# Differential attention, the first of two layers: three of eight query tiles transposed by VectorE instead of two, and the softmax ratio moved from VectorE to ScalarE

## The chip, the cores and the metric

The kernel runs on one core of one Trainium2 chip. The metric is device time in microseconds of one execution. A core has five engines that run their own instruction streams and wait for each other through semaphores: TensorE (PE in the profile; PEld is its loading of weights), VectorE (DVE), ScalarE (ACT), GpSimd (POOL) and SyncE (SP), which here only issues DMAs.

## The reference

Two transformer layers over X of shape (2, 1024, 128). The change touches only the attention of the first layer, a differential attention with 16 heads of width 64:

```
Q1, Q2 = halves of X Wq + bq      K1, K2 = halves of X Wk + bk      V = X Wv + bv
P  = softmax(Q1 K1' / 8) - lam * softmax(Q2 K2' / 8)
O  = P V ;  Y = concat_heads(O) Wo + bo ;  layer norm, times 0.2, and so on
```

After it come a mixture-of-experts feed-forward part, a second attention (16 heads of width 8) and a gated feed-forward part. They are the same in both kernels.

## The kernel before

**Tiling.** The first layer is a loop over `n` from 0 to 31: `n = 2 * head + batch`. Each n has 8 steps `s`, one for each tile of 128 queries. In a step, TensorE computes two fills of scores (`scores(n, s, p)`, p = 0 for Q1K1, p = 1 for Q2K2), each 128 queries x 1024 keys in two PSUM banks. A fill is numbered v = 2s + p within n. Three pairs of banks serve as a ring (`ring(v)`), and a fill waits until the exponential that read its pair two or three fills ago is done. Once per n the ring skips a place so that the pair 0 takes the projection of Q for the next n (`project_q`), and the pair 2 the output product. Q and K are split in a high and a low float16 part (`high_q`, `high_k` on ScalarE write the high part from PSUM, `low_q`, `low_k` on VectorE the rest), and a fill is three products of them.

**The way of a tile.** VectorE takes the negative maximum of a fill over the keys (`maximum`, line 1152). ScalarE takes the exponential with that as bias and leaves the row's sum (`exponent`, line 847). When both exponentials of a tile are there, VectorE takes the reciprocals of the two sums (`weigh`, line 1159) and the ratio rho = lam * sum1 / sum2 (line 1161). GpSimd scales the second exponential by rho and subtracts it from the first (`subtract`, lines 655 and 656). The result, still to be divided by sum1, is transposed so that it can be multiplied by V:
- six of the eight tiles (`BY_PE`) by TensorE, in two runs of four 128x128 transposes into one PSUM bank (`turn(n, s, i)`, line 1585), each run evacuated by ScalarE (`keep_t`, line 858). Tile s is turned in step s + 3.
- two tiles, 0 and 2 (`BY_DVE`), by VectorE in 32x32 blocks (`turn_blocks`, line 1204), in steps 3 and 5; SyncE stores the blocks to DRAM and loads them back in their places (`store_blocks`, `load_turned`).

**The values.** The product with V of n - 1 (`values`, line 1599) runs as 8 pieces in steps 3 to 6 of n: `PIECES` gives pieces 0, 1, 2 to step 3, piece 3 to step 4, pieces 4, 5, 6 to step 5 and piece 7 to step 6. In step 3 they stand between the fills v6 and v7. VectorE divides by the first sum, spread over partitions by DMA (`normalise`, step 7).

**Order.** Every engine's order is written out by hand in loops over n and s; there is no planner. In a step, VectorE's order before the change is: maximum of the first fill, `weigh` of the tile before, maximum of the second fill, then what else the step has: in step 2 `low_q(n + 1)` behind the second maximum, in steps 3 and 5 `turn_blocks`. Ahead of the first maximum stand `normalise` in step 7 and `keep_v` in step 0. `low_k` stands in steps 1 and 2 between the maxima. The fill v7 waits for `low_q(n + 1)`, as it uses the pair that held Q's projection. ScalarE's order in a step is: `keep_t` of one half, first exponential, `keep_t` of the other half, second exponential, with `high_k` in steps 1 and 2 and `high_q` (line 871) in step 2. GpSimd's order is the eight `subtract`, and behind tile 4 of every even n `part_w`, the five small operations that prepare the next head's weights; in the first four n it has further preparation (`prepare`). An exponential of tile s + 4 writes into the buffer of tile s, so it waits until that tile is turned.

Of the kernel before, what the change touches and what calls it, by code (L numbers as in the profile page):

```python
# [28 lines left out]
def two_layers(nc, a, out):  # L29
    ctx = ExitStack()  # L30
    with ctx:
# [308 lines left out]
        BY_DVE = (0, 2)  # L340
# [42 lines left out]
        def _(sp):  # L383
# [81 lines left out]
            def store_blocks(n, i):  # L465

                sp.wait_ge(s_bt_ok, 2 * n + i + 1)
                if n >= 1:
                    sp.wait_ge(s_ptr_dma[(n - 1) % 2], 64 * ((n - 1) // 2 + 1))
                for j in range(4):  # L470
                    sp.dma_start(ptd[i].rearrange("(m p) (b c) -> p m b c", m=4, b=4)[:, :, j, :],
                                 stage[i][32 * j:32 * j + 32, :].rearrange("p (m c) -> p m c", m=4)).then_inc(s_ptw_dma, 16)

            def load_turned(n, i):

                sp.wait_ge(s_ptw_dma, 64 * (2 * n + i + 1))
                if n >= 2:
                    sp.wait_ge(s_pv_mm, n - 1)
                elif n == 1:
                    sp.wait_ge(s_wprep_ev, 6)  # L480
                at = 4 * BY_DVE[i]
                for k in range(2):
                    sp.dma_start(PT[2 * n % 3][k][:, at:at + 4, :, :], ptd[i].rearrange(
                        "p (b k c q) -> p b k c q", b=4, k=2, c=4)[:, :, k, :, :]).then_inc(s_ptr_dma[n % 2], 16)
# [8 lines left out]
            for n in range(-1, last0 + 1):  # L493
# [28 lines left out]
                if own:  # L522
                    store_blocks(n, 0)
                    spread_r(n, 0)
                    load_turned(n, 0)
                    store_blocks(n, 1)
                    load_turned(n, 1)
# [89 lines left out]
        def _(pool):  # L617
# [32 lines left out]
            def subtract(n, s):  # L650

                q = 8 * n + s
                e1, e2 = E1[s % 4], E2[s % 4]
                pool.wait_ge(s_rho_ok, q + 1)
                link(P.tensor_scalar(e2, e2, rho[:, s:s + 1], 1.0, ALU.mult, ALU.mult))  # L655
                P.tensor_tensor(e1, e1, e2, ALU.subtract).then_inc(s_sub_ok, 1)  # L656
# [62 lines left out]
            scale_q(0)  # L719
            for n in range(last0):  # L720
# [82 lines left out]
        def _(act):  # L803
# [33 lines left out]
            def exponent(n, s, p):  # L837
# [3 lines left out]
                if p == 0:  # L841
                    prev, tile = (n, s - 4) if s >= 4 else (n - 1, s + 4)
                    if tile in BY_DVE:
                        act.wait_ge(s_bt_ok, 2 * prev + BY_DVE.index(tile) + 1)
# [5 lines left out]

            def keep_t(n, s, i):
# [3 lines left out]
                if s in (1, 4) and i == 0:  # L855
                    at_least(act, s_pv_mm, n - 1 + half)
# [17 lines left out]
            for n in range(-1, last0 + 1):  # L874
                prv, own, nxt = n >= 1, 0 <= n < last0, n + 1 < last0
                for s in range(8):
# [19 lines left out]
                    if own:  # L896
                        exponent(n, s, 0)
                    if 3 <= s < 6 and n == 0:
# [178 lines left out]
        def _(dve):  # L1077
# [77 lines left out]
            def weigh(n, b, s):  # L1155
# [41 lines left out]
            def turn_blocks(n, i):  # L1197

                dve.wait_ge(s_sub_ok, 8 * n + BY_DVE[i] + 1)
# [19 lines left out]
            for n in range(-1, last0):  # L1219
                prv, own, nxt = n >= 1, 0 <= n < last0, n + 1 < last0  # L1220
                for s in range(8):
# [8 lines left out]
                    if n == 0 and s == 1:  # L1230
                        dve.wait_ge(s_ld_l0, 48)
# [280 lines left out]
        def _(pe):  # L1512
# [75 lines left out]
            def values(n, j):  # L1588
# [4 lines left out]
                if j == 0:  # L1593
                    pe.wait_ge(s_ptr_dma[n % 2], 64 * (n // 2 + 1))
# [97 lines left out]
            PIECES = {3: (0, 1, 2), 4: (3,), 5: (4, 5, 6), 6: (7,)}  # L1692
# [429 lines left out]
```

## Time and profile before

Three runs took 1572.45, 1575.74 and 1575.19 us: the median is 1575.19. The profiled execution took 1573.77 us; its trace has a span of 1572.0 us from the first to the last instruction.

| | busy us | share of the span |
|---|---|---|
| TensorE (matmul) | 1439.6 | 92% |
| VectorE | 1376.4 | 88% |
| ScalarE | 1198.3 | 76% |
| GpSimd | 1003.8 | 64% |

The mean granted clock of TensorE is 0.967 of full speed. The chain of work that ended last lies for 53% on TensorE, 14% on ScalarE, 13% on VectorE and 7% on GpSimd; 11% of it is issue. The first layer's attention takes about the first 1060 us of the span, and GpSimd's work lies almost all in it. In timelines, the first number is the start in us from the span's start, the second the busy time; a pair in square brackets is the idle time of that engine before it and what released it. Successive operations on an engine overlap a little, so what an operation costs is better read from one start to the next.

### The profile page before, as it was taken

The page shows a single profiled execution, that of the slowest core. Times are in us where ns is not written, and L with a number is a line of the kernel's source. Part 1 is how long each engine was busy: PE and PEld are TensorE (multiplying, and loading weights), DVE is VectorE, ACT ScalarE, POOL GpSimd, SP SyncE. Part 2 cuts the span into 40 slices and gives each one's busy share as a digit, 9 for nine tenths or more (in the row PEclk, how much of TensorE's full clock was granted, in tenths as well). Part 3 has the DMA queues.
Part 4 walks back from the last instruction along what each step waited for, and adds up shares of the span by engine and source line. Part 5 has one row for each costly group of instructions (what it writes and reads, how often), then busy time and mean ns, then how long its engine had stood idle before and what let it go on. Part 6 is the DMA issues. An engine that isn't in the chain of part 4 may idle for free.

```text
span 1572.0 us, 28031 instructions
## 1 busy us (share of the span) xinstructions
PE 1439.6 (92%) x10243; PEld 588.5 (37%) x10243; DVE 1376.4 (88%) x2107; ACT 1198.3 (76%) x1911; POOL 1003.8 (64%) x727
## 2 busy tenths in 40 slices
PE   5899999999999999999999999986685999999985
PEld 1434443344434443344334433434541222222223
DVE  6798998999899989999999989988687999999947
ACT  4787888888888888888888888874342888888882
POOL 2999998898898988989889889880032011111112
PEclk9999999999999999999999999997696999999997
DMA  4243433343244323433343333420000110000001
GB/s 126 76 105 92 106 86 82 102 112 90 78 103 110 96 77 104 109 92 85 91 107 105 83 91 93 114 68 1 1 22 21 31 35 15 16 16 16 16 16 34
DMA packets 154641, 110.80 MB, mean 70 GB/s; under 512 B 31381, under 2 KB 142906, under 8 KB 154506
## 3 DMA queue, kind: packets, MB, share of 16 engines
q1 hardware_dynamic: 154378, 108.99, 26.5%
q8 instruction: 82, 1.34, 0.4%
q14 instruction: 53, 0.43, 0.1%
q0 software_dynamic: 128, 0.03, 0.0%
HBM read 53.82 MB, written 34.87 MB: 56 GB/s over the span
## 4 chain that ended last, share of the span: by engine, by line
PE 53%; ACT 14%; DVE 13%; issue 11%; POOL 7%; DMA 1%; SPq 0%; POOLq 0%; ACTq 0%; DVEq 0%
PE PS L1573 14%; PE PS L1585 10%; PE PS L1599 9%; ACT ering L847 7%; PE PS L1980 4%; POOL ering L656 3%; DVE nmx L1152 2%; PE PS L1942 2%; DVE region L1172 2%; PE PS L1632 2%; PE PS L1964 2%; ACT region L871 2%; DVE mxp L1479 2%; ACT ering L1059 2%; POOL ering L655 2%
## 5 line engine op out<-in xcount | busy, mean ns | idle before, releaser
L1152 DVE TENSOR_REDUCE nmx<-PS 128x1 f32<-128x1024 f32 x512 | 620.1, 1216 | 54.4 <-PE PS L1574 53.5
L847 ACT ACTIVATE ering<-PS,nmx 128x1024 f32<-128x1024 f32 x512 | 570.6, 1116 | 109.6 <-DVE nmx L1152 109.5
L656 POOL TENSOR_TENSOR ering<-ering 128x1024 f32<-128x1024 f32 x256 | 604.2, 2360 | 21.4
L1573 PE MATMUL PS<-region 64*128 64x512 f16 x1536 | 405.1, 381 | 20.4 <-ACT ering L847 14.5
L1574 PE MATMUL PS<-region 64*128 64x512 f16 x1536 | 405.2, 381 | 0.0
L655 POOL TENSOR_SCALAR ering<-ering,rho 128x1024 f32<-128x1024 f32 x256 | 287.3, 1122 | 95.2 <-DVE rho L1161 94.5
L1479 DVE TENSOR_REDUCE mxp<-PS 128x2 f32<-128x1024 f32 x256 | 304.2, 1222 | 34.3 <-PE PS L1964 29.9
L1059 ACT ACTIVATE ering<-PS 128x1024 f32<-128x1024 f32 x256 | 259.6, 1024 | 70.0 <-PE PS L1942 64.1
L1585 PE MATMUL PS<-ident,ering 128*128 128x128 f32 x1536 | 251.5, 286 | 15.6 <-ACT t L858 8.1
L1585 PEld LDWEIGHTS PS<-ident,ering 128*128 128x128 f32 x1536 | 161.6, 141 | 201.7 <-issue 73.8
L1573 PEld LDWEIGHTS PS<-region 64*128 64x128 f16 x1536 | 112.6, 94 | 261.3 <-ACT ering L847 110.2
L1980 PE MATMUL PS<-ering,acc 128*32 128x256 f32 x2048 | 160.5, 391 | 5.0 <-ACT ering L1059 1.5
L761 POOL TENSOR_TENSOR on<-osb,rcp 128x512 f32<-128x512 f32 x16 | 20.4, 1276 | 155.3 <-DMA rcp<-scr 155.3
L1574 PEld LDWEIGHTS PS<-region 64*128 64x128 f16 x1536 | 112.5, 94 | 0.0
L1599 PE MATMUL PS<-t,region 128*64 128x512 f32 x224 | 108.3, 608 | 0.0
L1599 PE MATMUL PS<-region 128*64 128x512 f32 x216 | 104.5, 609 | 0.0
L847 ACT ACTIVATION_READ_ACCUMULATOR ering<-PS,nmx 128x1 f32 x512 | 104.1, 203 | 0.0
L858 ACT ACTIVATE t<-PS 128x512 f32<-128x512 f32 x132 | 78.9, 598 | 28.0 <-PE PS L1585 27.2
L858 ACT ACTIVATE region<-PS 128x512 f32<-128x512 f32 x124 | 74.1, 598 | 20.5 <-PE PS L1585 19.7
L1204 DVE STREAM_TRANSPOSE t<-ering 128x1024 f32<-128x1024 f32 x64 | 79.0, 1234 | 0.0
L1161 DVE TENSOR_SCALAR rho<-sums,rr,cols 128x1 f32<-128x1 f32 x256 | 69.9, 273 | 9.3
L779 POOL TENSOR_TENSOR yT<-yT,yc 128x512 f32<-128x512 f32 x12 | 15.2, 1270 | 88.5 <-ACT yc L1040 88.5
(301 smaller groups left out, 1876.2 us busy)
## 6 DMA issues: line engine op xcount, KB each, us to landing
ptd<-t SPq DMA_DIRECT2D x256, 128.0 KB, 2.4
region<-region SPq DMA_DIRECT2D x64, 256.0 KB, 3.5
t<-ptd SPq DMA_DIRECT2D x44, 256.0 KB, 3.5
region<-ptd SPq DMA_DIRECT2D x44, 256.0 KB, 3.5
va<-ptd SPq DMA_DIRECT2D x20, 256.0 KB, 3.4
acc<-ptd SPq DMA_DIRECT2D x20, 256.0 KB, 3.5
osb<-scr SPq DMA_DIRECT2D x32, 128.0 KB, 3.3
rcp<-scr SPq DMA_DIRECT2D x32, 128.0 KB, 3.3
```

The source lines that it names most:

```text
L655: link(P.tensor_scalar(e2, e2, rho[:, s:s + 1], 1.0, ALU.mult, ALU.mult))
L656: P.tensor_tensor(e1, e1, e2, ALU.subtract).then_inc(s_sub_ok, 1)
L847: A.activation((E1, E2)[p][s % 4], PS[:, bank:bank + 2, :].rearrange("p a b -> p (a b)"), ACT.Exp, bias=nmx[:, 2 * s + p:2 * s + p + 1], s ...
L858: A.activation(PT[(2 * n + half) % 3][i][:, at:at + 4, :, :].rearrange("p b k q -> p k b q"), TRB.rearrange("p (k b q) -> p k b q", k=4, b ...
L1059: A.activation(ering[:, c % 8, :, :], PS[:, at:at + 2, :], ACT.Exp, scale=SCALE1).then_inc(s_exps1, 1)
L1152: V.tensor_reduce(nmx[:, 2 * s + p:2 * s + p + 1], PS[:, bank:bank + 2, :].rearrange("p a b -> p (a b)"), AX.X, ALU.max, negate=True).then ...
L1479: V.reduce_max(part[:, 2 * hp:2 * hp + 2, qt, kh:kh + 1], PS[:, at:at + 2, :], AX.X).then_inc(s_maxed1, 1)
L1573: MM(PS[:, bank, :], top[0:64, ql, q], KT[b][0:64, p, kl, :], start=(j == 0), stop=(j == 2))
L1574: mm = MM(PS[:, bank + 1, :], bottom[64:128, ql, q], KT[b][64:128, p, kl, :], start=(j == 0), stop=(j == 2))
L1585: mm = TR(TRB[:, j * 128:j * 128 + 128], E1[s % 4][:, k * 128:k * 128 + 128], ident[:, :])
L1599: mm = MM(MISC[64 * half:64 * half + 64, :], vt, PT[(2 * n + half) % 3][j // 4][:, :, j % 4, :], start=(j == 0), stop=(j == 7))
L1980: mm = MM(OT[32 * i:32 * i + 32, at], vst[:, n % 2, k, i, :], ering[:, c % 8, i // 2, at], start=(k == 0 and half == 0), stop=(k == 7 and ...
```

## The change

- `BY_DVE` becomes (0, 1, 2): tile 1 too is transposed by VectorE, in step 4, and no longer by TensorE and ScalarE. The two staging buffers and DRAM buffers are used in turn by the three tiles, with the waits that this takes.
- The ratio leaves VectorE's `weigh`. ScalarE makes sum1 / sum2 (`ratio`), behind the first exponential of the next step. Lambda is applied by GpSimd, as second factor of its scaling, where there was 1.0.
- `low_q(n + 1)` moves from the end of step 2 to step 3, behind the first maximum and ahead of `weigh`.
- `PIECES` moves piece 4 of the values from step 5 to step 4.
- The wait for the constants (`s_ld_l0`) moves from VectorE's first steps to GpSimd, ahead of its loop.

```diff
-        BY_DVE = (0, 2)
+        BY_DVE = (0, 1, 2)
...
             def store_blocks(n, i):
-                sp.wait_ge(s_bt_ok, 2 * n + i + 1)
-                if n >= 1:
-                    sp.wait_ge(s_ptr_dma[(n - 1) % 2], 64 * ((n - 1) // 2 + 1))
+                c = len(BY_DVE) * n + i
+                sp.wait_ge(s_bt_ok, c + 1)
+                if c >= 2:
+                    sp.wait_ge(s_ptr_dma[c % 2], 32 * (c // 2))
...
                     store_blocks(n, 0)
                     spread_r(n, 0)
                     load_turned(n, 0)
-                    store_blocks(n, 1)
-                    load_turned(n, 1)
+                    for i in range(1, len(BY_DVE)):
+                        store_blocks(n, i)
+                        load_turned(n, i)
...
-                link(P.tensor_scalar(e2, e2, rho[:, s:s + 1], 1.0, ALU.mult, ALU.mult))
+                link(P.tensor_scalar(e2, e2, rho[:, s:s + 1], cols[:, LAM:LAM + 1], ALU.mult, ALU.mult))
...
+            pool.wait_ge(s_ld_l0, 48)
             for n in range(last0):
...
+            def ratio(n, s):
+                act.wait_ge(s_rr_ok, 8 * n + s + 1)
+                A.activation(rho[:, s:s + 1], sums[:, s, 0:1], ACT.Identity, scale=rr[:, n % 2, 1, s:s + 1],
+                             bias=0.0).then_inc(s_rho_ok, 1)
...
                     if own:
                         exponent(n, s, 0)
+                    if own if s else prv:
+                        ratio(n if s else n - 1, (s + 7) % 8)
...
                 V.reciprocal(rr[:, b, :, s], sums[:, s, :]).then_inc(s_rr_ok, 1)
-                dve.wait_ge(s_rr_ok, q + 1)
-                V.tensor_scalar(rho[:, s:s + 1], sums[:, s, 0:1], rr[:, b, 1, s:s + 1], cols[:, LAM:LAM + 1], ALU.mult,
-                                ALU.mult).then_inc(s_rho_ok, 1)
...
             def turn_blocks(n, i):
+                c = len(BY_DVE) * n + i
                 dve.wait_ge(s_sub_ok, 8 * n + BY_DVE[i] + 1)
-                if n == 0:
+                if c < 2:
                     dve.wait_ge(s_xt_mm, 4)
                 else:
-                    dve.wait_ge(s_ptw_dma, 64 * (2 * n + i - 1))
-                V.transpose(stage[i].rearrange("p (m k q) -> p k m q", m=4, k=8),
+                    dve.wait_ge(s_ptw_dma, 64 * (c - 1))
+                V.transpose(stage[c % 2].rearrange("p (m k q) -> p k m q", m=4, k=8),
                             E1[BY_DVE[i]].rearrange("p (k m q) -> p k m q", m=4, k=8)).then_inc(s_bt_ok, 1)
...
                         maximum(n, s, 0)
-                    if n == 0 and s == 1:
-                        dve.wait_ge(s_ld_l0, 48)
+                    if s == 3 and nxt and own:
+                        low_q(n + 1)
...
-                    if s == 2 and nxt and own:
-                        low_q(n + 1)
-                    if own and s in (3, 5):
-                        turn_blocks(n, s // 2 - 1)
+                    if own and s - 3 in BY_DVE:
+                        turn_blocks(n, BY_DVE.index(s - 3))
...
-            PIECES = {3: (0, 1, 2), 4: (3,), 5: (4, 5, 6), 6: (7,)}
+            PIECES = {3: (0, 1, 2), 4: (3, 4), 5: (5, 6), 6: (7,)}
```

The loads and the waits of the values on them follow the same count c; the first of the tiles that TensorE turns in the lower half is now tile 3, and it carries the wait for a free buffer that tile 1 had.

## Rows read from the trace of the kernel before

**Rows 1.** Busy time by engine in three stretches: us, engines (x), clock, DMA share, GB/s.

```profile
50.00:200.00 150.00, 142.44 (x960) 62.08 (x962) 133.15 (x193) 121.78 (x216) 142.47 (x129) 1.00 0.35 92
528.19:559.96 31.77, 31.09 (x208) 12.96 (x206) 29.12 (x41) 26.69 (x48) 27.76 (x16) 1.00 0.38 96
559.96:591.72 31.76, 31.09 (x208) 12.95 (x206) 29.11 (x41) 26.69 (x47) 29.34 (x21) 1.00 0.37 94
```

**Rows 2.** Timeline of ScalarE, line 871: start, us, engine, line, shapes, [idle before].

```profile
36.38 1.11 ACT L871 ACTIVATE region<-PS,small 128x1024 f16<-128x1024 f32 x1
...
175.15 1.11 ACT L871 ACTIVATE region<-PS,small 128x1024 f16<-128x1024 f32 x1
...
1001.10 1.11 ACT L871 ACTIVATE region<-PS,small 128x1024 f16<-128x1024 f32 x1
```

**Rows 3.** Timeline of VectorE, one head-batch, steps 3 to 6 (columns as before).

```profile
557.51 1.28 DVE L1172 SCALAR_TENSOR_TENSOR region<-PS,small,region 128x1024 f16<-128x1024 f32 x1 [0.99 <-ACT region L871]
...
560.22 1.21 DVE L1152 TENSOR_REDUCE nmx<-PS 128x1 f32<-128x1024 f32 x1
561.35 1.23 DVE L1204 STREAM_TRANSPOSE t<-ering 128x1024 f32<-128x1024 f32 x1
562.51 1.18 DVE L1152 TENSOR_REDUCE nmx<-PS 128x1 f32<-128x1024 f32 x1
563.62 0.14 DVE L1159 RECIPROCAL rr<-sums 128x2 f32<-128x2 f32 x1
563.80 0.27 DVE L1161 TENSOR_SCALAR rho<-sums,rr,cols 128x1 f32<-128x1 f32 x1
...
569.33 1.22 DVE L1152 TENSOR_REDUCE nmx<-PS 128x1 f32<-128x1024 f32 x1
```

**Rows 4.** Timeline of TensorE's matmuls, the same stretch.

```profile
555.85 0.39 PE L1573 MATMUL PS<-region 64*128 64x512 f16 x1
...
559.33 0.39 PE L1573 MATMUL PS<-region 64*128 64x512 f16 x1
...
561.22 0.39 PE L1573 MATMUL PS<-region 64*128 64x512 f16 x1 [0.42 <-ACT ering L847]
...
561.97 0.66 PE L1585 MATMUL PS<-ident,ering 128*128 128x128 f32 x4
...
564.99 0.39 PE L1573 MATMUL PS<-region 64*128 64x512 f16 x1
...
587.61 0.39 PE L1573 MATMUL PS<-region 64*128 64x512 f16 x1
```

**Rows 5.** Timeline of ScalarE, the same stretch.

```profile
563.73 1.11 ACT L847 ACTIVATE ering<-PS,nmx 128x1024 f32<-128x1024 f32 x1 [0.47 <-DVE nmx L1152]
...
571.05 1.11 ACT L847 ACTIVATE ering<-PS,nmx 128x1024 f32<-128x1024 f32 x1
...
574.14 0.60 ACT L858 ACTIVATE t<-PS 128x512 f32<-128x512 f32 x1 [0.29 <-PE PS L1585]
```

**Rows 6.** Timeline of GpSimd, the same stretch.

```profile
564.17 1.12 POOL L655 TENSOR_SCALAR ering<-ering,rho 128x1024 f32<-128x1024 f32 x1 [0.21 <-DVE rho L1161]
...
576.57 1.12 POOL L655 TENSOR_SCALAR ering<-ering,rho 128x1024 f32<-128x1024 f32 x1
```

**Rows 7.** Timeline of TensorE's weight loads, the same stretch.

```profile
577.04 0.42 PEld L1585 LDWEIGHTS PS<-ident,ering 128*128 128x128 f32 x4 [0.76 <-POOL ering L656]
```

**Rows 8.** Groups of ScalarE by line and shape: busy us, mean ns, idle before.

```profile
L858 ACT ACTIVATE t<-PS 128x512 f32<-128x512 f32 x12 | 7.2, 598 | 1.9 <-PE PS L1585 1.8
L865 ACT ACTIVATE region<-PS,small 128x512 f16<-128x512 f32 x4 | 2.8, 692 | 0.0
```

**Rows 9.** Timeline of ScalarE near the start.

```profile
5.93 0.19 ACT L829 ACTIVATE small<-PS 128x16 f32<-128x16 f32 x1 [3.93 <-PE PS L1521]
6.01 0.18 ACT L830 ACTIVATE small<-PS 128x16 f32<-128x16 f32 x1
```

**Rows 10.** The page's DMA issues: line, count, KB each, median us to landing.

```profile
ptd<-t SPq DMA_DIRECT2D x256, 128.0 KB, 2.4
```

More of the change, by code:

```diff
@@ L465, in store_blocks @@
             def store_blocks(n, i):
-                sp.wait_ge(s_bt_ok, 2 * n + i + 1)
-                if n >= 1:
-                    sp.wait_ge(s_ptr_dma[(n - 1) % 2], 64 * ((n - 1) // 2 + 1))
+                c = len(BY_DVE) * n + i
+                sp.wait_ge(s_bt_ok, c + 1)
+                if c >= 2:
+                    sp.wait_ge(s_ptr_dma[c % 2], 32 * (c // 2))
                 for j in range(4):
-                    sp.dma_start(ptd[i].rearrange("(m p) (b c) -> p m b c", m=4, b=4)[:, :, j, :],
-                                 stage[i][32 * j:32 * j + 32, :].rearrange("p (m c) -> p m c", m=4)).then_inc(s_ptw_dma, 16)
+                    sp.dma_start(ptd[c % 2].rearrange("(m p) (b c) -> p m b c", m=4, b=4)[:, :, j, :],
+                                 stage[c % 2][32 * j:32 * j + 32, :].rearrange("p (m c) -> p m c", m=4)).then_inc(s_ptw_dma, 16)
             def load_turned(n, i):
-                sp.wait_ge(s_ptw_dma, 64 * (2 * n + i + 1))
+                c = len(BY_DVE) * n + i
+                sp.wait_ge(s_ptw_dma, 64 * (c + 1))
                 if n >= 2:
@@ L482, in load_turned @@
                 for k in range(2):
-                    sp.dma_start(PT[2 * n % 3][k][:, at:at + 4, :, :], ptd[i].rearrange(
-                        "p (b k c q) -> p b k c q", b=4, k=2, c=4)[:, :, k, :, :]).then_inc(s_ptr_dma[n % 2], 16)
+                    sp.dma_start(PT[2 * n % 3][k][:, at:at + 4, :, :], ptd[c % 2].rearrange(
+                        "p (b k c q) -> p b k c q", b=4, k=2, c=4)[:, :, k, :, :]).then_inc(s_ptr_dma[c % 2], 16)
             def swap_q(m):
@@ L843, in exponent @@
                     if tile in BY_DVE:
-                        act.wait_ge(s_bt_ok, 2 * prev + BY_DVE.index(tile) + 1)
+                        at_least(act, s_bt_ok, len(BY_DVE) * prev + BY_DVE.index(tile) + 1 if prev >= 0 else 0)
                     else:
@@ L854, in keep_t @@
                 act.wait_ge(s_tr_mm, turned(n, s) + i + 1)
-                if s in (1, 4) and i == 0:
+                if s in (3, 4) and i == 0:
                     at_least(act, s_pv_mm, n - 1 + half)
@@ L1197, in turn_blocks @@
             def turn_blocks(n, i):
+                c = len(BY_DVE) * n + i
                 dve.wait_ge(s_sub_ok, 8 * n + BY_DVE[i] + 1)
-                if n == 0:
+                if c < 2:
                     dve.wait_ge(s_xt_mm, 4)
                 else:
-                    dve.wait_ge(s_ptw_dma, 64 * (2 * n + i - 1))
-                V.transpose(stage[i].rearrange("p (m k q) -> p k m q", m=4, k=8),
+                    dve.wait_ge(s_ptw_dma, 64 * (c - 1))
+                V.transpose(stage[c % 2].rearrange("p (m k q) -> p k m q", m=4, k=8),
                             E1[BY_DVE[i]].rearrange("p (k m q) -> p k m q", m=4, k=8)).then_inc(s_bt_ok, 1)
@@ L1593, in values @@
                 if j == 0:
-                    pe.wait_ge(s_ptr_dma[n % 2], 64 * (n // 2 + 1))
+                    c = len(BY_DVE) * n + len(BY_DVE) - 1
+                    for i in range(2):
+                        pe.wait_ge(s_ptr_dma[i], 32 * ((c - i) // 2 + 1))
                 if j % 4 == 0:
```

## The prediction

> **What bounds the kernel now.** I read the windows first. In a steady stretch the first layer's loop spends 31.77 us on one head-batch (one head of one batch, n in the code), and TensorE is busy for 31.09 of them, VectorE 29.1, GpSimd 27.8 where n is odd and 29.3 where it is even, ScalarE 26.7, all at the full granted clock of 1.00 [rows 1]. The reader is to see two things: TensorE has 0.7 us of idle time at most, and GpSimd, which looks idle on average, is nearly as full in every second head-batch. The even ones carry `part_w`. In the first 150 us GpSimd is busy 142.47 of 150, as much as TensorE.
>
> Second, the period. ScalarE writes Q's high part once per n. Its start moves from 36.38 to 175.15 in four periods (34.7 us each) and from 175.15 to 1001.10 in 26 periods (31.77 each) [rows 2]. So whatever the change is worth in a steady period counts some 27 times, and the first four have a bound of their own.
>
> Third, the timelines of one even period, read side by side [rows 3 to 7]. I give offsets from 555.85, where TensorE starts the scores of tile 3's first half (v6 below: fills are numbered 2s + p); the next v6 is at 587.61, 31.76 later [rows 4]. The chain to see: v7 starts at 3.48, behind three value pieces; its maximum on VectorE starts at 4.37, then tile 0 is turned at 5.50, the maximum of v8 starts at 6.66 [rows 3], its exponential on ScalarE at 7.88 [rows 5], and v11, which needs that exponential's PSUM pair, starts at 9.14 [rows 4]. After v11 TensorE is nearly dense to the next v6.
>
> **The change part by part.** The sum is made against the profiled execution, 1573.77 us (span 1572.0); the median of the runs shown, 1575.19, is 1.42 above it.
>
> *Turning tile 1 leaves TensorE.* Two runs of four transposes go, 0.66 busy each, 0.6 apart from start to start [rows 4]: 1.2 us less per period, and the value piece moved from step 5 into step 4 fills part of the place. But this work stood between v9 and v10, ahead of v11, and v11 waits for the chain above, in which nothing moves: v7 is still behind three value pieces, tile 0 is still turned before the maximum of v8. So v11 stays at 9.14 and TensorE idles about 1.1 us before it. What TensorE does win is the moved value piece, 0.9 us less between v11 and v12.
>
> *Q's low part later.* Today VectorE idles 0.99 us before it, waiting for ScalarE [rows 3]. The maximum of v6 goes ahead of it and fills the gap. The low part then ends near 3.3, just ahead of v7 at 3.48. The 0.42 us wait of TensorE at v9 [rows 4] goes too, but what is late next is v11, at its old time. So this edit is worth 0 in a steady period. If its cover fails (low part after 3.48), v7 and everything behind it slips by the difference, which I bound at 0.2.
>
> *VectorE from v11 on.* Each of the 8 ratio operations goes. The ratio starts 0.18 behind the reciprocal and lasts 0.27 [rows 3]; the next operation starts 0.08 before the end, as behind a maximum (1.21 long, 1.13 to the next start), so the pair costs 0.37. The reciprocal alone, 0.14 long, I put at 0.13: 0.24 goes per tile. Between the maximum of v8 (6.66) and that of v12 there are now 1.11 + 0.13 + 1.13 + 1.16 and 1.13 + 0.13 + 1.13 + 1.16 = 7.08, from the start-to-start times of a maximum (1.13) and a turning (1.16) [rows 3]. That puts v12's maximum at 13.74, where it was 13.48 [rows 3]: the added turning eats the TensorE gain, and VectorE is never idle from 4.4 to there. Its exponential starts 1.24 later, 14.98; it was 15.20 [rows 5], because ScalarE was then waiting for TensorE. So 0.2 us is won here, and about 0.45 at the evacuation that waited 0.29 for TensorE at 574.14 [rows 5].
>
> *The ratio on ScalarE.* The trace has no such form. A copy of 128x512 takes 598 ns and the same with one pointer operand 692 [rows 8], so a pointer costs 94; the small copy takes 0.19 and the next starts 0.08 behind it [rows 9]. From these the ratio takes 0.28 and occupies ScalarE for 0.18; the ends are 0.08 (no pointer cost, full overlap) and 0.28 (no overlap). ScalarE loses two evacuations (0.49 each) and gains 8 ratios: 1.44 less 0.98, 0.5 us busier per period, harmless at 26.7 of 31.8 except where it paces. It paces in steps 7 to 1, where one or two ratios lie on its way: 0.1 of the 0.45 is given back. An odd period becomes 31.4, that is -0.37.
>
> [...]
>
> *Where the ratio now stands.* This decides the sign. Before, tile 3's ratio followed the maximum of v8 and GpSimd started tile 3's scaling at 8.32, waiting for it (0.21 idle) [rows 6]. Now it stands behind the exponential of v8: 7.88 + 1.10 + 0.28 + 0.10 = 9.36. GpSimd starts 1.04 later. From that start it goes without a gap through tiles 3, 4, `part_w` and 5: 12.40 to 576.57 [rows 6]. The turning of tile 5 on TensorE starts at 21.19, only 0.47 behind that [rows 7]. With n even it can now start at 9.36 + 12.40 + 0.08 = 21.84, where TensorE would want it at 20.74. From there to the next v6 it was 10.57; with one ratio on ScalarE's way 10.64. An even period becomes 32.5, that is +0.71. With n odd there is no `part_w` (1.8 us) and GpSimd is in time.
>
> *Lambda as a second pointer on GpSimd.* Not in the trace for this engine; between 0 and 0.1 per tile (a pointer's price on ScalarE [rows 8]); I take 0, keeping 0.1 x 3 per even period (+4 us) for the range. The wait for the constants moves off VectorE at the start and is long met: 0.
>
> *DMA.* A third tile adds 4 stores and 2 loads per n, and two stage buffers now serve three turnings. Tile 0 is turned by 6.7 and its stores land 2.4 us after issue [rows 10], near 11 with four issues in a row and the semaphores; tile 2 is turned at 12.5: hidden, with 1.5 to spare. Counting store, wait and load three times over I have the last load landed near 28; the values want it at 32.5. The queue is a third busy [rows 1]: 0. If the cover fails, VectorE stops in front of tile 2 with v12's maximum queued behind it.
>
> *Sum.* First four periods: GpSimd paces [rows 1, 2], the ratio comes late once: +1.0. Then 13 even periods x 0.71 = +9.2; 14 others x -0.37 = -5.2. Total +5.0: 1578.8 for a profiled execution, 1580.2 for the median. The likeliest case's own range, with the ratio's price, is 1576 to 1585.
>
> **The rivals.**
> *The freed TensorE time comes through* (0.07): 32 x 1.2 = -38, 1537. For it: 31.09 of 31.77 busy. Against it: v11's wait, which doesn't contain what was removed.
> *GpSimd doesn't decide* (0.20), the other side: even periods gain like odd ones, 27 x -0.37 + 1 = -9, 1566. It needs GpSimd's tile 5 to be ready by 20.7, against 21.8 in my sum; it holds if the exponential of v8 starts a microsecond earlier than before or tile 3's ratio is not held behind it.
> *Balance* (0.20): the ratio occupies 0.08 only. Then odd -0.6, even +0.55, sum near 0, 1575.
> *ScalarE is worse* (0.15): no overlap, or waits for the reciprocal; odd -0.15, even +0.9: +11, 1586. Decides from 0.28 us per ratio.
> That the change doesn't do what it says would be a third tile whose load holds up the values; the 4 us to spare speak against it, and I put it into the last case.
>
> **How the numbers follow.** Forecast 0.38, rivals 0.07, 0.20, 0.20, 0.15. A difference under 0.2% (3.15 us) can't be told from none. Faster: the first two rivals and a part of the balance, 0.29. Within: most of the balance and the lower edge of the forecast, 0.26. Slower: 0.45. The range runs from 1563 (the second rival with some margin) to 1592 (the last, with lambda's pointer), leaving out the first rival and a little above.
>
> **What would show it.** In the changed trace: v11 about 9.1 behind v6, after an idle of 1 us; no idle before Q's low part; GpSimd's tile 3 starting 9.3 to 9.4 behind v6; TensorE waiting about a microsecond for GpSimd at tile 5 where n is even and not at all where it is odd; periods that alternate 32.5 and 31.4. I am wrong if the periods are equal, if v11 comes before 9, or if the ratio takes less than 0.2 us.

## The result, and the profile after

The changed kernel takes 1580.98 us (median of 6 runs, 1579.48 to 1584.73) against 1574.5 us for the kernel before (median of 6, 1572.45 to 1575.74). The ratio is 1.0045, with a 95% interval of 1.0032 to 1.0057: slower by about 0.45%. The profiled execution has a span of 1579.1 us in a run of 1580.95 us; before it was 1572.0 in 1573.77. So there are 7.1 us to account for. One of the twelve executions of the kernel with lambda left out (experiment 2) took 2582.82 us and is left out of that kernel's ratio.

The page of the changed kernel, with the busy shares, the shares of the chain that ended last, and the groups in which something moved (busy us, mean ns, idle before and its releaser):

```profile
PE 1405.5 (89%) x9987; PEld 563.1 (36%) x9987; DVE 1334.5 (85%) x1883; ACT 1203.1 (76%) x2103; POOL 1024.9 (65%) x727
...
PE 40%; POOL 19%; issue 17%; DVE 12%; ACT 11%; DMA 1%; SPq 0%; POOLq 0%; ACTq 0%; DVEq 0%
...
L1581 PE MATMUL PS<-region 64*128 64x512 f16 x1536 | 405.8, 381 | 34.8 <-ACT ering L851 29.9
...
L658 POOL TENSOR_SCALAR ering<-ering,rho,cols 128x1024 f32<-128x1024 f32 x256 | 307.6, 1202 | 82.8 <-ACT rho L858 82.0
...
L1593 PE MATMUL PS<-ident,ering 128*128 128x128 f32 x1280 | 211.6, 288 | 45.2 <-POOL ering L659 30.9
...
L858 ACT ACTIVATE rho<-sums,rr 128x1 f32<-128x1 f32 x256 | 77.2, 302 | 0.1
```

TensorE has lost 34 us of work (1439.6 before, 10,243 matmuls) and yet the program is longer. The reader is to look at the idle columns: in front of the turnings on TensorE (L1593) 30.9 us are now spent waiting for GpSimd, where the page of the kernel before shows 8.1 us of waiting for ScalarE as the most. In front of GpSimd's scaling (L658) 82.0 us are spent waiting for the ratio. That is less in all than before, when GpSimd waited 94.5 us for VectorE's ratio; what has changed is where the waits stand. GpSimd has 19% of the chain. It had 7% before. The scaling itself takes 1202 ns where it took 1122. The scores (L1581) wait 29.9 us for an exponential, 14.5 before: that is mostly v11.

Now the stretches, as in [rows 1], over the first periods, one even and one odd period, and the whole steady part from the start of the one Q high part (`high_q`) to the other:

```profile
50.00:200.00 150.00, 133.76 (x886) 56.48 (x886) 124.20 (x158) 118.47 (x233) 142.21 (x126) 0.99 0.44 121
561.49:594.16 32.67, 29.94 (x202) 12.09 (x198) 27.78 (x34) 26.79 (x54) 29.79 (x22) 1.00 0.46 126
594.16:625.28 31.12, 29.83 (x202) 12.08 (x198) 27.79 (x34) 26.79 (x54) 28.59 (x17) 1.00 0.49 132
178.69:1008.08 829.39, 777.03 (x5152) 314.29 (x5148) 722.66 (x859) 696.73 (x1379) 759.32 (x482) 1.00 0.47 128
```

An even period takes 32.67 us and an odd one 31.12, where both took 31.77 [rows 1, 2]. The 26 steady periods add 829.39 - 825.95 = 3.4 us. The first four take 178.69 - 37.17 = 141.5 instead of 138.8 [rows 2], 2.7 more; `high_q` starts 0.8 later in the first of them; 0.1 is left behind the last. That is the 7.1.

The timelines of an even period of the changed kernel (start, us, engine, line, form, [idle before]) answer to [rows 3 to 7]. v6 starts at 560.89 here, and offsets are again from v6. TensorE:

```profile
560.89 0.39 PE L1581 MATMUL PS<-region 64*128 64x512 f16 x1
...
564.37 0.39 PE L1581 MATMUL PS<-region 64*128 64x512 f16 x1
...
570.01 0.39 PE L1581 MATMUL PS<-region 64*128 64x512 f16 x1 [0.91 <-ACT ering L851]
...
582.96 0.66 PE L1593 MATMUL PS<-ident,ering 128*128 128x128 f32 x4 [1.48 <-POOL ering L659]
...
593.57 0.39 PE L1581 MATMUL PS<-region 64*128 64x512 f16 x1
```

VectorE:

```profile
562.89 1.27 DVE L1181 SCALAR_TENSOR_TENSOR region<-PS,small,region 128x1024 f16<-128x1024 f32 x1
...
567.53 1.19 DVE L1164 TENSOR_REDUCE nmx<-PS 128x1 f32<-128x1024 f32 x1
568.64 0.15 DVE L1171 RECIPROCAL rr<-sums 128x2 f32<-128x2 f32 x1
568.71 1.20 DVE L1164 TENSOR_REDUCE nmx<-PS 128x1 f32<-128x1024 f32 x1
...
574.43 1.19 DVE L1164 TENSOR_REDUCE nmx<-PS 128x1 f32<-128x1024 f32 x1
```

ScalarE:

```profile
568.75 1.11 ACT L851 ACTIVATE ering<-PS,nmx 128x1024 f32<-128x1024 f32 x1 [1.05 <-DVE nmx L1164]
...
569.86 0.28 ACT L858 ACTIVATE rho<-sums,rr 128x1 f32<-128x1 f32 x1
570.04 1.10 ACT L851 ACTIVATE ering<-PS,nmx 128x1024 f32<-128x1024 f32 x1
...
575.65 1.12 ACT L851 ACTIVATE ering<-PS,nmx 128x1024 f32<-128x1024 f32 x1
```

GpSimd:

```profile
565.07 1.20 POOL L658 TENSOR_SCALAR ering<-ering,rho,cols 128x1024 f32<-128x1024 f32 x1 [0.54 <-ACT rho L858]
...
570.24 1.20 POOL L658 TENSOR_SCALAR ering<-ering,rho,cols 128x1024 f32<-128x1024 f32 x1 [1.52 <-ACT rho L858]
...
577.49 0.31 POOL L633 TENSOR_SCALAR wq_s<-wq_raw 128x128 f32<-128x128 f32 x1
...
579.27 1.20 POOL L658 TENSOR_SCALAR ering<-ering,rho,cols 128x1024 f32<-128x1024 f32 x1
...
582.88 1.21 POOL L658 TENSOR_SCALAR ering<-ering,rho,cols 128x1024 f32<-128x1024 f32 x1
```

What to see: v11 at 570.01 is 9.12 behind v6, with 0.91 of idle time. Q's low part has no idle time before it. Tile 3's scaling starts 9.35 behind v6 and had to wait 1.52 us for its ratio. From there GpSimd runs without a gap through tiles 3, 4, `part_w` (577.49 to 579.27) and 5, and TensorE stands still for 1.48 us until tile 5 is scaled, at 582.96.

### The profile page after: what moved, and what is told of

The parts are those of the page before. It is cut to its first block, busy times and chain, and to the rows that moved or that the text cites. A ratio compares the mean times of both kernels' runs of the same rounds, so it can differ in the third digit from the quotient of the medians.

```text
span 1579.1 us, 27745 instructions
## 1 busy us (share of the span) xinstructions
PE 1405.5 (89%) x9987; PEld 563.1 (36%) x9987; DVE 1334.5 (85%) x1883; ACT 1203.1 (76%) x2103; POOL 1024.9 (65%) x727
## 2 busy tenths in 40 slices
DMA packets 206866, 144.36 MB, mean 91 GB/s; under 512 B 34453, under 2 KB 195130, under 8 KB 206730
## 4 chain that ended last, share of the span: by engine, by line
PE 40%; POOL 19%; issue 17%; DVE 12%; ACT 11%; DMA 1%; SPq 0%; POOLq 0%; ACTq 0%; DVEq 0%
PE PS L1581 9%; POOL ering L659 8%; PE PS L1609 7%; ACT ering L851 6%; PE PS L1593 6%; POOL ering L658 5%; PE PS L1990 4%; DVE nmx L1164 2%; DVE t L1214 2%; PE PS L1642 2%; PE PS L1952 2%; PE PS L1974 2%; DVE mxp L1487 2%; PE PS L1670 1%; ACT ering L1071 1%
## 5 line engine op out<-in xcount | busy, mean ns | idle before, releaser
L1581 PE MATMUL PS<-region 64*128 64x512 f16 x1536 | 405.8, 381 | 34.8 <-ACT ering L851 29.9
L658 POOL TENSOR_SCALAR ering<-ering,rho,cols 128x1024 f32<-128x1024 f32 x256 | 307.6, 1202 | 82.8 <-ACT rho L858 82.0
L1593 PE MATMUL PS<-ident,ering 128*128 128x128 f32 x1280 | 211.6, 288 | 45.2 <-POOL ering L659 30.9
L1581 PEld LDWEIGHTS PS<-region 64*128 64x128 f16 x1536 | 112.4, 94 | 295.1 <-ACT ering L851 121.7
L1593 PEld LDWEIGHTS PS<-ident,ering 128*128 128x128 f32 x1280 | 135.6, 142 | 195.0 <-POOL ering L659 111.2
L1214 DVE STREAM_TRANSPOSE t<-ering 128x1024 f32<-128x1024 f32 x96 | 118.3, 1232 | 0.0
L851 ACT ACTIVATION_READ_ACCUMULATOR ering<-PS,nmx 128x1 f32 x512 | 107.7, 210 | 0.0
L868 ACT ACTIVATE t<-PS 128x512 f32<-128x512 f32 x110 | 66.6, 606 | 22.0 <-PE PS L1593 21.3
L858 ACT ACTIVATE rho<-sums,rr 128x1 f32<-128x1 f32 x256 | 77.2, 302 | 0.1
L868 ACT ACTIVATE region<-PS 128x512 f32<-128x512 f32 x102 | 61.7, 605 | 16.0 <-PE PS L1593 15.4
```

The source lines that it names most:

```text
L658: link(P.tensor_scalar(e2, e2, rho[:, s:s + 1], cols[:, LAM:LAM + 1], ALU.mult, ALU.mult))
L851: A.activation((E1, E2)[p][s % 4], PS[:, bank:bank + 2, :].rearrange("p a b -> p (a b)"), ACT.Exp, bias=nmx[:, 2 * s + p:2 * s + p + 1], s ...
L1214: V.transpose(stage[c % 2].rearrange("p (m k q) -> p k m q", m=4, k=8), E1[BY_DVE[i]].rearrange("p (k m q) -> p k m q", m=4, k=8)).then_in ...
L1581: MM(PS[:, bank, :], top[0:64, ql, q], KT[b][0:64, p, kl, :], start=(j == 0), stop=(j == 2))
L1593: mm = TR(TRB[:, j * 128:j * 128 + 128], E1[s % 4][:, k * 128:k * 128 + 128], ident[:, :])
```

## The experiments

Each is an edit of the changed kernel, except the one named as an edit of the kernel before. The table has the medians, the ratio to the kernel before in the same session with its 95% interval, and the length of a steady even and odd period in the profiled execution. The kernel before had a median of 1574.5 in the session of the changed kernel, 1575.63 in that of the next four rows, and 1574.99 and 1573.79 in the two later ones. So rows of different sessions are best compared by their ratios.

```
                                            us       ratio [95%]              even   odd
kernel before                               1574.5   1                        31.77  31.77
changed kernel                              1580.98  1.0045 [1.0032, 1.0057]  32.67  31.12
part_w behind tile 2                        1560.83  0.9905 [0.9890, 0.9921]  31.13  31.13
the same in the kernel before               1577.28  1.0012 [0.9998, 1.0026]  31.77  31.77
lambda left out of the scaling              1580.26  1.0021 [1.0011, 1.0030]  32.41  31.12
ratio back on VectorE                       1583.19  1.0050 [1.0037, 1.0063]  32.03  32.04
tile 1 back on TensorE                      1592.22  1.0110 [1.0096, 1.0123]  32.66  31.78
tile 1 back, part_w behind tile 2           1578.01  1.0019 [1.0010, 1.0028]  31.78  31.78
low part back in step 2                     1582.19  1.0048 [1.0035, 1.0062]  32.63  31.12
low part back, part_w behind tile 2         1581.77  1.0046 [1.0033, 1.0058]  32.61  31.12
tile 3's ratio alone on VectorE             1586.63  1.0076 [1.0064, 1.0089]  32.75  31.38
part_w behind tile 2, a piece behind v11    1573.75  1.0001 [0.9992, 1.0010]  31.64  31.64
part_w behind tile 2, a piece before v11    1557.95  0.9895 [0.9880, 0.9911]  31.16  30.98
```

**1. `part_w` moved out of GpSimd's run.** My theory puts all the loss on GpSimd's run in even periods. So the 1.8 us of `part_w` were put where GpSimd waits anyway, ahead of tile 3.

```diff
-                    if s == 4 and b == 0 and h + 1 < H0:
+                    if s == 2 and b == 0 and h + 1 < H0:
                         part_w
```

> The changed kernel with part_w (the five small GpSimd operations for the next head's weights, even n only) moved from behind tile 4 to behind tile 2, where GpSimd now idles 1.5 us waiting for tile 3's ratio. Theory (GpSimd's queue from tile 3 to tile 5 sets the even periods): even periods fall from 32.67 to about 31.2, like the odd ones (31.12); 13 or 14 of them, so about -20 us, 1560. Rival A (the even periods are longer because their DMAs or ScalarE's extra work delay TensorE): no change, 1580. Rival B (part_w itself costs 1.8 us wherever it stands): no change, 1580, with the wait moved to tile 3.

The even period fell from 32.67 to 31.13, the length of the odd one, and the time to 1560.83. 13 x (32.67 - 31.13) = 20.0 us; the medians differ by 20.2, and by the ratios it is 22 us. GpSimd in that kernel (v6 at 550.89):

```profile
555.08 1.19 POOL L658 TENSOR_SCALAR ering<-ering,rho,cols 128x1024 f32<-128x1024 f32 x1 [0.59 <-ACT rho L858]
...
558.70 0.30 POOL L633 TENSOR_SCALAR wq_s<-wq_raw 128x128 f32<-128x128 f32 x1
...
560.47 1.19 POOL L658 TENSOR_SCALAR ering<-ering,rho,cols 128x1024 f32<-128x1024 f32 x1
...
571.34 1.19 POOL L658 TENSOR_SCALAR ering<-ering,rho,cols 128x1024 f32<-128x1024 f32 x1
```

Tile 5 is now done at 571.3, 20.4 behind v6 instead of 22.0. TensorE turns it without a wait, at 571.42, so it comes with only 0.1 us to spare. So the stall for GpSimd was all that set the even periods apart. The same edit of the kernel before:

> Control: the same move of part_w in the kernel before, where tile 5 was ready 0.47 us before TensorE took it. Theory: GpSimd had slack there, so nothing: 1574 to 1575, periods 31.77 for both parities. Rival B or one that makes part_w costly by itself: a change of the same size as in the changed kernel.

There it brought nothing, as expected: 31.77 in both periods. Before the change tile 5 was ready 0.47 us ahead of its turning [rows 6, 7]; after it TensorE waits 1.48 us. (The profile of this control has one early period of 36.76 us, where the kernel before has 32.88; see the last section.)

**2. Lambda's pointer.** The ratio isn't multiplied by lambda here.

```diff
-                link(P.tensor_scalar(e2, e2, rho[:, s:s + 1], cols[:, LAM:LAM + 1], ALU.mult, ALU.mult))
+                link(P.tensor_scalar(e2, e2, rho[:, s:s + 1], 1.0, ALU.mult, ALU.mult))
```

> The changed kernel with GpSimd's second factor 1.0 instead of the pointer to lambda (lambda is left out of the computation). Theory: the scaling falls from 1.20 to 1.12 us; even periods lose 3 x 0.08 = 0.24 us each (13 times: -3.2), and the first four periods, which GpSimd paces, 32 x 0.08 = -2.6; odd periods nothing. Total about -6 us, 1575. Rival (the pointer's 0.08 us is hidden, as GpSimd idles 1.5 us in every period): 0, 1580.

The scaling takes 1119 ns without the pointer and 1202 with it. The even period fell by 0.26 (three scalings in the run: 0.25), the odd one not at all. 13 x 0.26 = 3.4 us, and something in the first periods, were due. The ratio fell from 1.0045 to 1.0021, which is 3.8 us; the intervals, 1.0032 to 1.0057 and 1.0011 to 1.0030, nearly touch, so the total supports the sum but can't test it closely. The medians themselves differ by 0.7 only, but they come from two sessions. The profiled execution has one early period of 36.7 us instead of 32.6, again the matter of the last section. How often that happens in the others isn't known.

**3. The parts one by one.** First the ratio back on VectorE with lambda in it, and three tiles kept. GpSimd's second factor is 1.0 again, so this kernel is also rid of lambda's pointer on GpSimd, and VectorE waits for the constants as before the change.

```diff
-                link(P.tensor_scalar(e2, e2, rho[:, s:s + 1], cols[:, LAM:LAM + 1], ALU.mult, ALU.mult))
+                link(P.tensor_scalar(e2, e2, rho[:, s:s + 1], 1.0, ALU.mult, ALU.mult))
...
-                    if own if s else prv:
-                        ratio(n if s else n - 1, (s + 7) % 8)
...
+                dve.wait_ge(s_rr_ok, q + 1)
+                V.tensor_scalar(rho[:, s:s + 1], sums[:, s, 0:1], rr[:, b, 1, s:s + 1], cols[:, LAM:LAM + 1], ALU.mult,
+                                ALU.mult).then_inc(s_rho_ok, 1)
...
+                    if n == 0 and s == 1:
+                        dve.wait_ge(s_ld_l0, 48)
```

> The changed kernel with the ratio, lambda in it, back on VectorE as before the change; three tiles turned by VectorE, Q's low part later, pieces as changed. Theory: tile 3's scaling starts at 8.3 us behind v6 again and the stall at tile 5 goes, while VectorE's chain from v8's to v12's maximum is 0.6 us longer; both parities near 31.6, total about 1571. Rival C (the third tile with its DMAs and VectorE's load is what costs, not the ratio's place): as slow as the changed kernel, 1580 or more. Rival D (VectorE's chain was not what paces odd periods): odd stay at 31.1, and the total falls to 1560.

That was a miss by 12 us. The part on GpSimd was right: TensorE's waits for it at the turnings shrank from 30.9 to 3.4 us, and the even period fell by 0.64. But the odd one rose by 0.92. VectorE in that kernel, from the maximum of v8 to that of v12:

```profile
569.10 1.19 DVE L1162 TENSOR_REDUCE nmx<-PS 128x1 f32<-128x1024 f32 x1
570.21 0.15 DVE L1169 RECIPROCAL rr<-sums 128x2 f32<-128x2 f32 x1
570.39 0.27 DVE L1171 TENSOR_SCALAR rho<-sums,rr,cols 128x1 f32<-128x1 f32 x1
570.59 1.21 DVE L1162 TENSOR_REDUCE nmx<-PS 128x1 f32<-128x1024 f32 x1
...
576.64 1.19 DVE L1162 TENSOR_REDUCE nmx<-PS 128x1 f32<-128x1024 f32 x1
```

Reciprocal and ratio take 0.38 from start to start where the reciprocal alone takes 0.07, and v12's maximum stands 7.54 behind v8's instead of 6.90. TensorE then waits, once more, for ScalarE:

```profile
571.58 0.39 PE L1584 MATMUL PS<-region 64*128 64x512 f16 x1 [0.91 <-ACT ering L851]
...
575.36 0.39 PE L1584 MATMUL PS<-region 64*128 64x512 f16 x1 [0.33 <-ACT ering L851]
```

The second wait, at v13, isn't in the changed kernel. Then the opposite: tile 1 back on TensorE (with the value pieces and the turn steps of before), and the ratio left on ScalarE.

```diff
-        BY_DVE = (0, 1, 2)
+        BY_DVE = (0, 2)
...
-            PIECES = {3: (0, 1, 2), 4: (3, 4), 5: (5, 6), 6: (7,)}
+            PIECES = {3: (0, 1, 2), 4: (3,), 5: (4, 5, 6), 6: (7,)}
```

> The changed kernel with only tiles 0 and 2 turned by VectorE and the value pieces as before; the ratio stays on ScalarE, lambda on GpSimd, Q's low part late. Theory: the ratio's late place alone makes tile 5 late on GpSimd where n is even (even periods near 32.7), and odd ones lie near 31.5, as TensorE has its 1.2 us back: total about 1586. Rival E (the third turned tile is what lengthens even periods): both parities alike, at or under 31.77, total under 1575.

Even periods took 32.66 and odd ones 31.78. So the late ratio is enough to stall the even periods; the third tile and its DMAs aren't needed for it, and the rival that blamed them is out. The time, 1592.22, was 6 us above the expected one: the odd periods gained nothing against 31.77. And this with `part_w` behind tile 2, so that GpSimd doesn't hide the rest:

> The same with part_w behind tile 2. Theory: even periods join the odd ones near 31.5, total about 1570: the ratio's move is a gain by itself once part_w doesn't stand in GpSimd's run from tile 3 to tile 5, and the third tile is worth the rest to 1561. Rival F (the third tile gives nothing once GpSimd keeps up): 1561 as with three tiles.

Both periods then take 31.78, as before within 0.01. Where GpSimd doesn't decide, the four cases are: two tiles with the ratio on VectorE 31.77, two with it on ScalarE 31.78, three with it on VectorE 32.03, three with it on ScalarE 31.13. Neither part gains anything alone; together they gain 0.64. My reading, which no run isolates, is that the third tile alone overloads VectorE, and that the ratio alone frees VectorE where it doesn't set the pace. My expectation of 1570 had credited the ratio with a gain of its own.

**4. Q's low part.**

```diff
-                    if s == 3 and nxt and own:
+                    if s == 2 and nxt and own:
                         low_q(n + 1)      (now behind maximum(n, s, 1), as before)
```

The line in brackets is shortened: the call stands where it stood in the kernel before.

> The changed kernel with Q's low part back at the end of step 2 and part_w where it was, behind tile 4. Theory: in this arrangement the late low part is worth nothing, since v11 and tile 3's start on GpSimd hang on v7's maximum, not on v6's: periods 31.1 and 32.7, total 1580 as the changed kernel. The 21 us that the low part was worth with part_w behind tile 2 came from tile 2's start on GpSimd alone. Rival G: the late low part is worth 0.4 to 0.8 us per period by itself, total 1592 or more.

In the changed kernel its place is worth nothing: 32.63 and 31.12, within 0.04 of the periods of the changed kernel. Together with the move of `part_w`:

> The changed kernel with part_w behind tile 2 and Q's low part back at the end of step 2. Theory: TensorE waits again 0.4 us or more at v9 and VectorE idles 1 us before the low part, but v7's maximum and v11 keep their time: periods 31.1, total 1561, no change against the kernel with the low part late. Rival G (the late low part is a gain of its own): the 0.42 us at v9 come back in each period, +11 us, 1572.

A miss by 21 us, and an instructive one. ScalarE and GpSimd in that kernel, v6 at 562.64:

```profile
566.83 1.11 ACT L851 ACTIVATE ering<-PS,nmx 128x1024 f32<-128x1024 f32 x1 [1.39 <-DVE nmx L1164]
...
567.94 0.28 ACT L858 ACTIVATE rho<-sums,rr 128x1 f32<-128x1 f32 x1
```

```profile
568.32 1.20 POOL L658 TENSOR_SCALAR ering<-ering,rho,cols 128x1024 f32<-128x1024 f32 x1 [2.04 <-ACT rho L858]
...
571.93 0.30 POOL L633 TENSOR_SCALAR wq_s<-wq_raw 128x128 f32<-128x128 f32 x1
...
573.70 1.19 POOL L658 TENSOR_SCALAR ering<-ering,rho,cols 128x1024 f32<-128x1024 f32 x1
```

```profile
577.39 0.66 PE L1593 MATMUL PS<-ident,ering 128*128 128x128 f32 x4 [1.35 <-POOL ering L659]
```

The early low part stands ahead of the maximum of v6. The exponential of v6 comes later, tile 2's ratio behind it at 567.94 (5.3 behind v6 instead of 3.8), and GpSimd starts tile 2 at 5.7 instead of 4.2. With `part_w` behind it, tile 3 starts at 11.1 instead of 9.6, and now the turning of tile 3 waits (1.35 us). The slack into which `part_w` fits exists only because the low part is late. That edit was worth nothing in the changed kernel and 1.5 us per even period in the better one.

**5. Which ratio holds GpSimd up?** Only tile 3's ratio was given to VectorE, right behind its reciprocal. `part_w` stays behind tile 4.

```diff
-                    if own if s else prv:
+                    if (own if s else prv) and s != 4:
                         ratio(n if s else n - 1, (s + 7) % 8)
...
+                if s == 3:
+                    dve.wait_ge(s_rr_ok, q + 1)
+                    V.tensor_scalar(rho[:, s:s + 1], sums[:, s, 0:1], rr[:, b, 1, s:s + 1], 1.0, ALU.mult,
+                                    ALU.mult).then_inc(s_rho_ok, 1)
```

> The changed kernel with one ratio of eight, tile 3's, made by VectorE in step 4 behind the reciprocal; part_w stays behind tile 4. Theory (the late start of tile 3 on GpSimd sets the even periods): tile 3 starts 8.3 behind v6 instead of 9.4, even periods fall from 32.67 to about 31.7; VectorE's chain gets 0.3 longer, so odd periods rise from 31.12 to about 31.4; total about 1571. Rival H (GpSimd is late for its load as a whole, 30 of 31.8 us, wherever tile 3 starts): even periods stay at 32.5 or more, total 1582.

Another miss: the even period rose to 32.75. GpSimd (v6 at 564.15), and ScalarE:

```profile
572.41 1.20 POOL L658 TENSOR_SCALAR ering<-ering,rho,cols 128x1024 f32<-128x1024 f32 x1 [0.41 <-DVE rho L1174]
...
577.22 1.20 POOL L658 TENSOR_SCALAR ering<-ering,rho,cols 128x1024 f32<-128x1024 f32 x1 [1.15 <-ACT rho L858]
...
586.22 1.20 POOL L658 TENSOR_SCALAR ering<-ering,rho,cols 128x1024 f32<-128x1024 f32 x1
```

```profile
575.73 1.11 ACT L851 ACTIVATE ering<-PS,nmx 128x1024 f32<-128x1024 f32 x1 [1.05 <-DVE nmx L1164]
...
576.83 0.28 ACT L858 ACTIVATE rho<-sums,rr 128x1 f32<-128x1 f32 x1
```

Tile 3 starts at 8.3, as in the kernel before. But then GpSimd waits 1.15 us for tile 4's ratio, which stands behind the exponential of v10 and starts 12.7 behind v6. Tile 5 is done at 22.1, against 22.0 without the edit. The prediction named tile 3's ratio as what anchors the run of GpSimd; the one of tile 4 anchors it at the same place, and in the changed kernel it is ready (573.31 + 0.28, 12.7 behind v6) only 0.3 us before tile 3 is finished. Both are late, and moving one alone moves only the wait. The odd period rose by 0.26, about the price of one ratio on VectorE's way (0.31).

**6. The value pieces.** With `part_w` moved, the 0.91 us of idle before v11 is the longest wait that is left on TensorE.

```diff
-            PIECES = {3: (0, 1, 2), 4: (3, 4), 5: (5, 6), 6: (7,)}
+            PIECES = {3: (0, 1), 4: (2, 3), 5: (4, 5, 6), 6: (7,)}
```

> The changed kernel with part_w behind tile 2 and value pieces 0,1 / 2,3 / 4,5,6 / 7 in steps 3 to 6 instead of 0,1,2 / 3,4 / 5,6 / 7. Theory: v7 starts when the low part ends, 3.33 instead of 3.48 behind v6, so v11 comes 0.15 earlier, but one more piece (0.9 us) stands behind v11 on TensorE, where there is 0.4 us of idle: between -4 and +10 us against 1561. If the place of v7 is what the period hangs on, -4; if TensorE's work behind v11 is, +8 or more.

Slower by 13 us than with the old pieces: 0.51 per period. One more piece stands behind v11, where TensorE is dense, while the hole before v11 stays at 0.91. And with only two pieces between v6 and v7, v7 now waits for Q's low part. Then with the piece left in front of v11:

```diff
+            PIECES = {3: (0, 1), 4: (2, 3, 4), 5: (5, 6), 6: (7,)}
```

> The changed kernel with part_w behind tile 2 and value pieces 0,1 / 2,3,4 / 5,6 / 7 in steps 3 to 6: one piece less between v6 and v7, one more between v9 and v10, where TensorE idles 1.3 us before v11. Theory: v7 starts at 3.33 (end of the low part) instead of 3.48, everything behind it 0.15 earlier, periods 31.0, total 1557. Rival (v11 was not held by v7's chain, and the idle time was needed by something else): v11 comes later by up to 0.9, total 1561 to 1585.

The time was 1557.95, the lowest of all. The hole before v11 is gone, and the one before v7 stands in its place:

```profile
555.50 0.39 PE L1581 MATMUL PS<-region 64*128 64x512 f16 x1 [0.65 <-DVE region L1181]
```

Even and odd periods take 31.16 and 30.98, 0.06 less on average than in experiment 1. The medians differ by 2.9, but the intervals of the ratios overlap, so that I claim no more than that it is not worse. This version beats the kernel before by 1.05% (0.89% to 1.20%).

## Why the prediction was right

The forecast was the right case: slower, by a stall of TensorE on GpSimd in every second period. That the number came so close, 1580.2 against 1580.98, is partly luck: two terms were off by some 2.5 and 3.6 us over the steady periods, in opposite directions. Point by point:

- *v11 stays where it was.* 9.14 was predicted, 9.12 measured, with 0.91 of idle time (1.1 predicted). Turning tile 1 off TensorE was swallowed there. Shown.
- *The low part costs and brings nothing.* It ends 3.3 behind v6, v7 starts at 3.48. Shown by experiment 4, for this kernel only.
- *VectorE from v11 on.* v12's maximum was put at 13.74 and stands at 13.54, mostly because the reciprocal takes 0.07 from start to start and not 0.13, twice on this way. ScalarE's exponential of v12 starts at 14.76, not 14.98. This is the likeliest mis-sized term in the odd periods: if the 0.22 is carried on whole to the next v6, it accounts for 0.22 of the 0.28 by which they came out shorter (-0.65 and not -0.37). No experiment isolates that. What VectorE was rid of per tile I had put at 0.24. Measured, the reciprocal alone takes 0.07 from start to start (its own record is 0.15 long) and the pair took 0.38 in experiment 3, so it was rid of 0.31. Of these, 0.11 are the ratio's wait for the reciprocal (0.18 behind its start instead of 0.07), and 0.20 lie between the ratio and the next operation. So the 0.24 of my sum was too low.
- *The ratio on ScalarE.* It lasts 0.28 and the next exponential starts 0.18 behind it (569.86, 570.04), both as derived from the copies [rows 8, 9].
- *GpSimd's run in even periods.* Predicted: tile 3 at 9.36, 12.40 to the end of tile 5, tile 5 turned at 21.84, then 10.64 to the next v6, 32.5 in all. Measured: 9.35, 12.64, 22.07, 10.61, 32.67. The 0.24 on the second term is lambda's pointer, which I took as 0: three times 0.08 (experiment 2). Experiment 1 shows that this stall is all of the even periods' loss. What I named as its origin, tile 3's ratio, is one of two: the ratio of tile 4 holds GpSimd at the same place (experiment 5).
- *The first four periods.* +1.0 predicted, +2.7 measured. GpSimd paces there, and the pointer costs it up to 32 x 0.08 = 2.6 us. In experiment 2 the first, third and fourth of these periods fall by 0.44, 0.81 and 0.27 without the pointer (39.75 to 39.31, 33.91 to 33.10, 35.30 to 35.03), 1.5 us of the 3.1 by which the change had lengthened these three; the second can't be compared. So the pointer accounts for about half. The cause of the rest is open, and each number comes from one profile.
- *The sum.* Steady +4.0 predicted (9.2 - 5.2), +3.4 measured: the rise of the even periods was put 0.19 too low and the fall of the odd ones 0.28 too small, and the two cancel in part. With the first periods 5.0 against 7.1; 0.8 of the difference is the later start of the first of them, which the sum didn't have.
- *DMA.* Traffic rose from 110.80 to 144.36 MB, and the page and the waits of the steady part show no wait of the values for a tile. Nothing was paid there, as predicted.

Of the rivals, the one in which the freed TensorE time comes through is out by v11's wait. *GpSimd doesn't decide* was wrong for this kernel, but experiment 1 made it true, and its number, 1566, was beaten by 5 us by the larger odd gain. *Balance*, which needed 0.08 us per ratio, and *ScalarE is worse*, which needed 0.28, are out by the measured 0.18.

## What to carry to other kernels

An engine that looks a third idle can be full in every second iteration. Before moving a producer later in its queue, follow what the consumer does from that moment up to the next point where somebody waits for it, and count every item in that run: here 1.0 us of lateness became 0.9 us per even period, and moving 1.8 us of unrelated work out of the run turned a loss of 6 us into a gain of 15. And try parts of a change together as well as alone: here the third tile and the ratio were each worth nothing or less without the other, `part_w`'s move was worth nothing without them, and the late low part nothing without `part_w`'s move.

## What the runs showed of the hardware

**Some VectorE operations beside an instruction of GpSimd lasted until that instruction had ended.** `weights_of_rows` runs once, at n = 1, s = 5: two TENSOR_SCALAR operations on VectorE, 128x256 f32 each. In the profiles they take between 0.57 us (the changed kernel) and 3.54 us (lambda left out) together; 3.45 in the kernel before with `part_w` moved. Where they are longest (2.72 us and more, three kernels), the period from n = 1 to n = 2 takes 36.6 to 36.8 us; with 1.44 us (tile 3's ratio alone on VectorE) it takes 35.07; in the nine other kernels, with 0.57 to 1.29 us, it takes 32.4 to 33.0. To test it, they were done four times over in the best version.

```diff
-                for k in range(2):
-                    ins = V.tensor_scalar(yc[:, k * M:k * M + M], fb[:, :], fcol[:, k:k + 1], None, ALU.is_equal)
-                link(ins)
+                for k in (0, 1) * 4:
+                    link(V.tensor_scalar(yc[:, k * M:k * M + M], fb[:, :], fcol[:, k:k + 1], None, ALU.is_equal))
```

> The version with part_w in step 2 and value pieces (0,1), (2,3,4), (5,6), (7), with the two TENSOR_SCALAR operations of weights_of_rows (VectorE, once, at n = 1, s = 5, 128x256 f32 each) done four times over: eight of them, each waiting for the one before. In the traces so far the pair took from 0.57 to 3.54 us together. Theory L (a lock): such a VectorE operation can't run while GpSimd runs one of its own on 128x1024 f32; it starts, and ends only when that GpSimd instruction ends (1.2 or 2.36 us long). Then most of the eight end within 0.4 us behind the end of a GpSimd instruction, they last 1.2 to 2.5 us each where they start beside one, 10 to 15 us for the eight, and the period from n = 1 to n = 2 grows by about as much; a GpSimd instruction may be 0.1 to 0.2 longer than its 1.20. Rival O (a cost paid once, as at the first use of a form): at most the first two are long, the other six take 0.3 us each, 2.5 to 5.5 us for all, and their ends have nothing to do with GpSimd's. [...] Run time by L about 1568, by O and S 1560 to 1563.

The one run took 1564.41 us, where 1568 was expected by theory L and 1560 to 1563 by its rivals; a single run decides little here, the trace does. The period from n = 1 to n = 2 went from 32.41 to 38.97. The eight on VectorE (durations min/median/max in ns, by stretch), and GpSimd beside them:

```profile
L1140 DVE TENSOR_SCALAR yc<-fb,fcol x8: 312/353/2394, 88.9 to 94.5; 128x256 f32<-128x256 f32 x8
```

```profile
89.36 1.32 POOL L658 TENSOR_SCALAR ering<-ering,rho,cols 128x1024 f32<-128x1024 f32 x1
90.76 2.34 POOL L659 TENSOR_TENSOR ering<-ering 128x1024 f32<-128x1024 f32 x1
98.37 1.20 POOL L658 TENSOR_SCALAR ering<-ering,rho,cols 128x1024 f32<-128x1024 f32 x1 [5.27 <-ACT rho L858]
```

The first two last 0.31 and 0.35. The third starts at 89.6, beside GpSimd's scaling, and lasts 1.18, to 90.8, 0.1 behind the scaling's end (90.68); the fourth starts at 90.9, beside the subtraction, and lasts 2.39, to 93.25, 0.15 behind the end of the subtraction (93.10). Then GpSimd has nothing to do, and the last four take 0.35 each. For the third and the fourth that is what theory L expects. A cost paid once is out: the third and the fourth are the long ones, and the first two are not. An even slowing of both engines, by which all eight would last about equally long, is out too: they last from 0.31 to 2.39. The sum of theory L, 10 to 15 us for the eight, was not reached: they took 5.9, since GpSimd ran dry and waited 5.27 us for a ratio behind them. The first scaling, with the end of the second of the eight beside it, took 1.32 instead of 1.20, so here GpSimd's instruction was the longer one for it. The trace shows who waits and for how long; what makes them wait no run shows. Not every operation of VectorE is touched: in the changed kernel all 512 maxima take 1.18 to 1.23 us, all 96 turnings 1.23 to 1.24 and all 256 reciprocals 0.14 to 0.17, beside GpSimd or not, and the old ratio, a TENSOR_SCALAR of 128x1, took 0.27 to 0.28 in all 256 cases. Whether the pair meets a gap of GpSimd's goes with a difference of up to 4 us in that period. That this is also what lengthened it in experiments 1 to 3 is inferred from one profile each; in all three, the longest operation of the pair (2.51, 2.52 and 2.45 us) ended 0.15 behind GpSimd's subtraction.

**A second pointer operand on GpSimd's scaling cost 0.08 us** for 128x1024 f32 (1202 ns with it, 1119 without, experiment 2), near the 94 ns that the prediction read for ScalarE from [rows 8].
